# A fused layer norm, attention and gated FFN kernel: another order of the steps within a head group's period

## The reference

```python
x = L0_attn_x                                   # (4, 512, 256)
xn = _layernorm(x, axis=-1)
Q = (xn @ Wq + bq).reshape(b, l, 16, 128)       # 16 query heads
K = (xn @ Wk + bk).reshape(b, l, 4, 128)        # 4 key heads, each used by 4 query heads
V = (xn @ Wv + bv).reshape(b, l, 4, 128)
scores = einsum('blhe,bmhe->bhlm', Q, K) / sqrt(128) + causal mask
ctx = einsum('bhlm,bmhe->blhe', softmax(scores), V)
y = gelu(ctx @ Wo + bo, approximate=False)
r = xn + y
s = (r - mean(r)) * rsqrt(var(r) + 1e-5) * gamma + beta
gate, up = split(xn @ w_gate_up.T)              # 2 x 1024 columns
g = silu((silu(gate) * up) @ w_down.T)
out = x + s * g
```

## Time and profile before

| | us |
|---|---|
| median of 3 runs | 644.49 |
| lowest, highest | 643.44, 648.06 |
| the profiled execution, its own time | 651.28 |
| its span, first to last instruction | 649.5 |
| TensorE busy in it | 609.5 (94%) |
| VectorE, ScalarE, GpSimd busy | 479.2, 428.7, 304.1 |

### The profile page before, as it was taken

The page is one execution under the profiler, slowest core; times in us unless marked ns, Lnnn a source line. Parts: engine busy times, 40 slices in busy tenths (PEclk is TensorE's granted clock), DMA queues, the critical chain, the costliest instruction groups (busy, mean ns, idle before and its releaser), DMA issues.

```text
span 649.5 us, 10475 instructions
## 1 busy us (share of the span) xinstructions
PE 609.5 (94%) x3342; PEld 525.8 (81%) x3342; DVE 479.2 (74%) x1087; ACT 428.7 (66%) x1023; POOL 304.1 (47%) x243
## 2 busy tenths in 40 slices
PE   6899999999799999999999999999999999999771
PEld 4688888888678889788988888897988989798650
DVE  5654556543888778778988787898878889887736
ACT  2434344534788688677978777797877879787440
POOL 0000000000055654555689645468964546897544
PEclk9999999999899999999999999999999999999786
DMA  7330221020487788876678888856798795779830
GB/s 240 129 130 33 66 97 62 3 73 10 143 236 212 200 227 245 227 221 164 176 191 251 252 224 219 214 170 188 228 267 232 195 247 155 204 227 269 216 100 32
DMA packets 72501, 113.28 MB, mean 174 GB/s; under 512 B 11136, under 2 KB 50176, under 8 KB 70400
## 3 DMA queue, kind: packets, MB, share of 16 engines
q1 hardware_dynamic: 71760, 112.30, 61.8%
q10 hardware_dynamic: 688, 0.33, 0.2%
HBM read 66.40 MB, written 46.20 MB: 173 GB/s over the span
## 4 chain that ended last, share of the span: by engine, by line
PE 62%; DMA 19%; DVE 7%; POOL 4%; ACT 4%; SPq 2%; issue 2%; ACTq 0%; POOLq 0%
PE bank L982 22%; PE down_ps L982 11%; DMA p_scratch<-probs 10%; PE down_ps L1112 8%; DMA probs<-p_scratch 7%; PE down_ps L1022 7%; PE bank L1011 6%; PE bank L1009 6%; POOL pT_lo L555 3%; DVE probs L915 3%; DMA raw<-in_wgu 2%; SPq L478 2%; PE bank L1073 2%; ACT pT_hi L698 1%; ACT probs L688 1%
## 5 line engine op out<-in xcount | busy, mean ns | idle before, releaser
L555 POOL TENSOR_TENSOR pT_lo<-probs,pT_hi 128x512 fp32r<-128x512 f32 x160 | 204.5, 1299 | 91.9 <-ACT pT_hi L698 91.4
L688 ACT ACTIVATE probs<-probs,least 128x512 f32<-128x512 f32 (+3 forms) x256 | 141.2, 554 | 37.6 <-DVE least L900 37.2
L900 DVE CUSTOM_DVE_ANT_0 probs<-bank,mask 128x512 f32<-128x512 f32 (+3 forms) x256 | 115.8, 484 | 24.9 <-PE bank L982 23.1
L698 ACT ACTIVATE pT_hi<-probs 128x512 fp32r<-128x512 f32 x160 | 96.1, 626 | 27.4 <-DMA probs<-p_scratch 21.1
L567 POOL TENSOR_TENSOR probs<-probs,inv 128x1024 f32<-128x1024 f32 (+1 forms) x32 | 47.0, 1469 | 141.1 <-DVE inv L908 141.0
L915 DVE STREAM_TRANSPOSE probs<-probs 128x2048 f32<-128x2048 f32 (+1 forms) x64 | 95.6, 1493 | 0.3 <-POOL probs L567 0.3
L1112 PE MATMUL down_ps<-wo_lo,cT_hi 128*128 128x256 f32 x256 | 74.4, 291 | 6.4 <-DVE cT_lo L940 6.3
L1112 PE MATMUL down_ps<-wo_hi,cT_lo 128*128 128x256 f32 x256 | 72.6, 284 | 0.0
L1112 PE MATMUL down_ps<-wo_hi,cT_hi 128*128 128x256 f32 x256 | 72.5, 283 | 0.0
L982 PE MATMUL down_ps<-pT_lo,v_hi 128*128 128x512 f32 x160 | 66.8, 417 | 6.0 <-POOL pT_lo L555 5.9
L982 PE MATMUL bank<-kT_lo,qT_hi 128*128 128x384 f32 (+1 forms) x192 | 66.4, 346 | 4.9 <-DVE least L900 3.3
(11 more groups left out here) (124 smaller groups left out, 1414.5 us busy)
## 6 DMA issues: line engine op xcount, KB each, us to landing
p_scratch<-probs SPq DMA_DIRECT2D x16, 1024.0 KB, 4.4
probs<-p_scratch SPq DMA_DIRECT2D x64, 256.0 KB, 4.9
p_scratch<-probs SPq DMA_DIRECT2D x16, 768.0 KB, 6.8
probs<-p_scratch SPq DMA_DIRECT2D x64, 192.0 KB, 4.0
inv_b<-i_scratch SPq DMA_DIRECT2D x32, 256.0 KB, 5.0
p_scratch<-probs SPq DMA_DIRECT2D x16, 512.0 KB, 3.5
probs<-p_scratch SPq DMA_DIRECT2D x64, 128.0 KB, 4.6
p_scratch<-probs SPq DMA_DIRECT2D x16, 256.0 KB, 4.7
```

The costliest lines, as they stand in the source:

```text
L555: nc.gpsimd.tensor_tensor(lo[:].rearrange("p (a n) -> p a n", a=BLOCKS), turned(t, j), f32(hi[:]).rearrange("p (a n) -> p a n", a=BLOCKS), ...
L688: nc.scalar.activation(p, p, ACT.Exp, bias=least[:, u, g:g + 1], scale=-1.0, accum_out=total[:, n * T + t, g:g + 1]).then_inc(exp_done, 1)
L698: nc.scalar.activation(hi[:].rearrange("p (a n) -> p a n", a=BLOCKS), turned(t, j), ACT.Copy).then_inc(probsT_hi, 1)
L900: nc.vector.tensor_tensor_reduce(out=head_of(t, g), in0=ps[:, 0:(t + 1) * P].rearrange("p (k i) -> p k i", i=BLOCK), in1=mask_of(t), scale ...
```

## The change

The five strings are replaced by five others with the same steps in them. And the wait of the mask step for the mask's load, which stood at one named step, now stands at whichever mask step is first; that is the same step in both orders.

```diff
--- before.py
+++ after.py
@@ -50,29 +50,28 @@
 
 
 TENSOR_ORDER = """
-P3.2- S3.2 S3.3 P3.3- O0-- P2.0- P2.1- S2.0 S2.1 S1.0 S1.1 P2.2- O3- S2.2 S2.3 P1.0- S1.2 S1.3 S0.0 P1.1- S0.1
-S0.2 Q2+ S0.3 O2- V1@0 V3@0 K+ P0.0- V0@0 Q0+ Q1+ V2@0 O1- P3.0 Q3+ S3.0+ S3.1+ P3.1
+P3.2- S3.2 S3.3 P3.3- V3@0 O0-- P2.0- P2.1- S2.0 S2.1 S2.2 P2.2- S2.3 O3- S1.0 S1.1 P1.0- S1.2 S1.3 S0.0 P1.1-
+S0.1 O2- S0.2 S0.3 V2@0 V1@0 Q3+ P0.0- Q0+ V0@0 K+ Q1+ O1- P3.0 Q2+ S3.0+ P3.1 S3.1+
 """
 
 SCALAR_ORDER = """
-ch3-- ph1.0-- ph1.1-- gelu-@2 e2.0- ph0.0-- ch2-- e2.1- e2.2- e2.3- e1.1- e1.2- e1.3- e1.0- qh2 e0.1- ch1--
-e0.2- vh1@1 e0.0- e0.3- vh3@1 kh ph3.0- ph3.2- vh0@1 qh0 ph3.1- qh1 ch0-- ph3.3- vh2@1 qh3 e3.0 ph2.0- ph2.1-
-e3.1 e3.2 e3.3 ph2.2-
+ph2.0- ph2.1- e3.1 e3.2 e3.3 ph2.2- ch3- vh3@0 ph1.0- ph1.1- gelu-@1 e2.0 ph0.0- ch2- e2.1 e2.3 e2.2 e1.1 e1.2
+e1.3 e1.0 e0.1 e0.0 ch1- e0.2 e0.3 vh2@0 vh1@0 qh3+ qh0+ ph3.0 ph3.2 vh0@0 ph3.1 kh+ qh1+ ph3.3 qh2+ ch0- e3.0+
 """
 
 VECTOR_ORDER = """
-m2.3 m1.2 m1.3 cl2- m0.1 m0.0 tt2 ri1 m0.2 st-@1 m0.3 ri2 ql2+ va1@0 va3@0 vl1@0 ri0 tt1 cl1- vl3@0 va0@0 kl+
-vl0@0 tt0 ql0+ va2@0 ql1+ xn@3 ya0-@0 nm-@1 cl0- vl2@0 m3.0+ ql3+ m3.1+ m3.2+ m3.3+ c3 ri3+ ya1-@0 tt3+ cl3
-m2.0+ m2.1+ c2 m1.1+ m1.0+ m2.2+
+va2@1 st-@2 ri3- va1@1 ri2- vl2@1 ri0- tt1- vl1@1 cl1-- ql3 va0@1 ql0 vl0@1 nm-@2 xn-@0 kl tt0- ql1 ya0-@1 m3.0
+ql2 m3.1 cl0-- m3.2 m3.3 c3- va3@0 ya1-@1 tt3 vl3@0 cl3- m2.0 m2.2 m2.1 c2- m2.3 m1.0 m1.1 cl2- m1.2 m1.3 m0.0
+m0.1 tt2 ri1 m0.2 m0.3
 """
 
 POOL_ORDER = """
-pl2.2-- pl1.0-- pl1.1-- out2-@3 pl0.0-- res-@2 out3-@3 out4-@3 out5-@3 no1- root-@2 out6-@3 no0- pl3.0- pl3.2-
-pl3.1- pl3.3- out0-@2 out1-@2 out7-@3 pl2.0- pl2.1-
+pl3.3-- out7--@0 out0-@3 out1-@3 pl2.0-- pl2.1-- out2-@3 pl2.2-- pl1.0-- out3-@3 pl1.1-- pl0.0-- out4-@3 out5-@3
+res-@2 no1- root-@2 out6-@3 no0- pl3.0- pl3.2- pl3.1-
 """
 
 TRANSFER_ORDER = """
-IW2- ST--@1 W1- R2- W0- R1- LX@3 IR2- R0- IW3 W3 IR3 R3 W2
+R2- W0- IR3- R1- LX@3 IR2- R0- W3 R3 W2 IW3 IW2 W1 ST--@0
 """
 
 TILE_ROWS = "V va vh vl gelu ya xn st nm res root out LX ST".split()
@@ -891,7 +890,7 @@
                     _, n, t, g = step
                     ps = ring_ps[RING["S", n, t, g][0]]
                     dve.wait_ge(scores_done, SCORED["S", n, t, g])
-                    if step == ("m", 0, T - 1, 0):
+                    if MASKED[step] == 1:
                         dve.wait_ge(mask_in_sem, 16)
                     if n and t in BY_DRAM:
                         dve.wait_ge(probsT_split, PT_SPLIT["pl", n - 1, t, t])
```

## The result

| | before | after |
|---|---|---|
| median of 6 runs each, us | 646.55 (643.44 to 649.06) | 653.04 (651.07 to 656.70) |
| ratio, after to before | 1 | 1.0103, 95% interval 1.0073 to 1.0134 |
| the profiled execution, and its span | 651.28, 649.5 | 656.12, 654.3 |
| TensorE busy, 190 to 596 us | 401.32 | 395.57 |

The changed kernel is 1% slower: 6.5 us by the medians, 4.8 us between the two profiled executions. The forecast was +2.5 us and 647.0, in a range of 639 to 653.

The account below looks back on a forecast made before the run. TensorE's own work, 26.8 us a period, was taken as the bound, with a transfer loop close behind. The terms 9.0 - 5.0 - 1.5 gave +2.5 us, so the median goes from 644.5 to 647.0, range 639 to 653.

Parts of the forecast that it names:

- The bound: TensorE's own work, 26.8 us a period, and close to it a loop through transfers, `R 2` and the exponentials.
- `xn` and `nm` ahead of `kT_lo`: S 3.0 waits for `kT_lo` in six periods, 1.9 us behind `nm`, 1.1 behind `xn`: +9.0 us.
- What it sets off: Waits at P 2.0 shrink in five of six periods (-5.0 us); those for `qT_lo` at S 3.3 go (-1.5).
- End: End of the run, chain through the last W 2 in the same order: 0, bounds -0.5 and +1 us.
- The sum: Whole kernel: 9.0 - 5.0 - 1.5 = +2.5 us, median from 644.5 to 647.0; chance 0.42.
- `IR 3`: Its load, moved behind `W 0`, lands at 29.5 where `c 3` is due at 29.7: cost 0, little in hand.
- rival D: `IR 3` lands late, holds `c 3` and tt 3, 0.5 to 1 us in each of fourteen periods: 654 to 661; chance 0.18.
- The sign that was to tell it: Waits of `down_ps` for `inv_b` stay below 2 us in all; 5 and more would mean rival D.
- `kT_hi` later: `kT_hi` behind three `pT_hi` comes some 2.5 us later; cost 0 unless `R 3` is over 1 us later.
- the rest: e 0.g, tt 1 and `W 1` up to 1 us earlier without gain; `pl 2.2` put off by 1.3 us.
- B: No contention for `xn` and `nm` in the new place; S 3.0 waits 0 to 0.3 us: 643; chance 0.18.
- C: Loop gets shorter too: `R 3`, W 2, `R 2` land about 1 us earlier, `pT_lo` waits go: 634 to 639; chance 0.12.

Follow-up runs that it names:

- the fourth group: Runs on one chip, with the unedited changed kernel against the kernel before again: 654.20 us against 651.79, ratio 1.0039.
- the better version: Changed kernel with `xn` moved to where GpSimd is idle and `nm` behind the low parts of keys and head 1: 649.75 us, ratio 0.9964 to the kernel before.

## Why the prediction was right and wrong

- **The bound.** Right: TensorE sets the pace, and its waits tell the rest. But its busy time in the long window, which was to stay near 401 us, fell to 395.57. The second bound close behind it, TensorE's waits for `pT_lo`, came back in nearly every version that took the waits at S 3.0 away.
- **`xn` and `nm` ahead of `kT_lo`.** The mechanism and its six places were right, and this is the step that failed, by its size. `xn` and `nm` were taken at 4.2 us each. `nm` took 4.29 and held S 3.0 by 1.8 (forecast 1.9). `xn` took 5.20, 5.37 and 5.20, because it started with GpSimd's four `pT_lo` (380.61 and 380.66 in period 7), where `nm` started 1.1 us behind them (442.49 and 441.41): each of the four pieces of `xn` waited out one of theirs, of `nm` only three. The delay behind `xn` was 1.78 to 1.95 where 1.1 was taken. The three `xn` made 5.5 us instead of 3.3, the three `nm` 5.4 instead of 5.7, and the term was 10.9 instead of 9.0. The price was read from period 15, where three `pT_lo` stood beside four pieces and one piece was short (371 ns). With four beside four it is about 4 x 1.3 = 5.2, an estimate from the same rows, and the range for this term should have gone up to that.
- **What it sets off.** Right in kind, 7.6 us instead of 6.5: all delays at P 2.0, P 2.1 and S 3.3 from period 1 on went, not five cases. Those at S 3.3 had been 2.5 us, where TensorE's own wait rows gave 1.5, and those at P 2.0 and P 2.1 5.3, where 5.0 was taken.
- **End.** Taken as 0, with a bound of +1; it was +1.36 in the profiled pair. W 2 of the last period took 7.81 us instead of 6.81. No run isolates this. In its second profile the changed kernel's end was shorter: 59.8 us from S 3.2 of period 15 to the last instruction, against 60.2 in the first and 58.8 before.
- **The sum.** With these sizes it is 10.91 - 7.59 + 1.36 + 0.16 = 4.84 instead of 2.5 us, the difference of the two profiled executions. The medians differ by 1.7 us more. The base was also low: 644.49 was the median of three runs, six gave 646.55. Of the 6.0 us between 647.0 and 653.04, about 2.1 are the base, 2.3 the terms, and 1.7 are left to the spread between executions. In the fourth group the change cost 2.4 us. That is the forecast's 2.5, but by luck: there only four delays at S 3.0 stood in the profile. The size of the effect is known to no better than 2 to 7 us; its sign was the same in both.
- **`IR 3`, rival D.** Cost 0 was right as far as two pairs in one group show (1.8 us more with `IR 3` back in the better version, 0.45 less in the changed kernel). The sign that was to tell it, waits for `inv_b` under 2 us, was 2.9 in the first profile and 8.8 in the second: the load does come late, and the time doesn't follow. In period 9 `R 2` landed at 449.44, `W 0` at 450.14 and `IR 3` behind both at 452.58, as rival D had it, and `c 3` started at 452.70; the price that D hung on it is not there.
- **`kT_hi` later, and the rest.** No delay of TensorE goes back to them: in periods without `xn` and `nm` S 3.0 was on time.
- **B and C.** B is refuted by the lengths of 4.29 and 5.2 us. C's first half came true where it didn't count: the waits for `pT_lo` went, but because TensorE came later.
- **The GPSIMD Engine Reference of the Trainium skill (Specifications).** It names the contention, and the trace agrees: 0.40 us a piece alone and up to 1.4 beside GpSimd. That section gives no price. In these traces a piece pays the rest of the GpSimd instruction that is running, and 0.15 us.

## What to carry to other kernels

A cheap instruction has the price of its place: ask what runs on the neighbouring engine during it, and count its pieces, not its size. Such work has two deadlines, the one behind it in its own queue and the one behind its consumer in the consumer's queue. The one version that came out below the kernel before (0.9964, compared once) met both, and those that looked only at the first handed the wait on. Where an order trades one wait for another within a loop that is nearly full, the total of one wait tells nothing; compare TensorE's delays step by step, in pairs run on one chip. And where two engines' work falls together by chance, take the price with full overlap as the upper end of the range.

## What the hardware did that was not expected

- Four pieces of VectorE's TENSOR_SCALAR (float32, 128x256) took 1.37 us where GpSimd was idle and 5.2 to 5.4 beside four GpSimd instructions of 1.3 us. With 128x128 they took 4.55: each piece waits for the end of the GpSimd instruction that is running, so it goes by the number of instructions. The kernel has no semaphore between these pieces, so the engines meet here too, and not only at semaphores, as the text ahead of the prediction has it.
- Not every VectorE instruction shows it. In the better version `kT_lo` and the transpose of `probs0` keep the lengths that they have where GpSimd is idle (0.73 to 0.74 and 0.69 to 0.70) while GpSimd was in its four `pT_lo` (440.76 to 445.97):

```profile
442.51 0.75 DVE L920 SCALAR_TENSOR_TENSOR kT_lo<-bank,bias,kT_hi 128x512 fp32r<-128x512 f32 x1 [0.59 <-ACT kT_hi L674]
443.18 0.70 DVE L914 STREAM_TRANSPOSE probs<-probs 128x512 f32<-128x512 f32 x1
```

- Nor is it this one instruction alone. At the end of the changed kernel one and the same step runs once without GpSimd and once (second line) beside it (third line), and takes twice as long; a plain TENSOR_TENSOR of 128x256 there goes from 0.42 to 0.83 us.

```profile
644.62 0.48 DVE L864 SCALAR_TENSOR_TENSOR res<-res,mv,rowc 128x256 f32<-128x256 f32 x1 [0.31 <-POOL rstd L583]
648.41 0.94 DVE L864 SCALAR_TENSOR_TENSOR res<-res,mv,rowc 128x256 f32<-128x256 f32 x1 [0.66 <-POOL rstd L583]
648.35 1.58 POOL L591 TENSOR_TENSOR res<-res,rowc 128x256 f32<-128x256 f32 x2
```

- 0.8 us in the landing of one read changed `xn` by 3.0 us. So the delays at S 3.0 differ from one execution of the same kernel to the next (six and four), and one profile of it is one sample. How much of the spread of its times comes from this isn't shown.
